# A GRU and an oscillator in one loop on one Trainium2 core: the first base's linear part by itself, pairs and gate work in another order

## What is computed

```python
x = x + GRU(cond_2048, x)                 # h_t from h_{t-1}: gates r, z, candidate n
x = x + Oscillator(cond_2048, cond_2048, x)
x = x + BlockAttention(x)                 # mean over blocks, one attention, layer norm
x = x + Resample(x, cond_2048)

# Oscillator, one time step (Runge-Kutta 4), DT = 0.01:
def derivative(q, p, drive):
    dq = q - q**3 / 3 - p + drive + tanh(q) @ coupling.T + bias
    dp = 0.08 * (q + 0.7 - 0.8 * p)
# dq1..dq4 at q, q + DT/2 dq1, q + DT/2 dq2, q + DT dq3
# q_next = clip(q + DT/6 (dq1 + 2 dq2 + 2 dq3 + dq4), -20, 20); p_next likewise
```

## Time and profile before

| | us |
|---|---|
| median of 3 runs (lowest, highest) | 3536.72 (3535.81, 3536.73) |
| the profiled execution, its own time | 3533.15 |
| its span | 3531.3 |
| busy PE, PEld | 3432.0, 3162.2 |
| busy DVE, ACT, POOL | 2842.0, 2612.1, 1536.1 |
| stage products L1193, first and last start | 210.5, 3390.1 |

### The profile page before, as it was taken

One profiled execution on the slowest core, in us unless ns is written; L12 is line 12 of the kernel. 1 busy time (PEld: TensorE's weight loads), 2 busy tenths in 40 slices (PEclk: granted clock), 3 DMA queues, 4 the chain that ended last, 5 costly groups with the idle time before them and its releaser, 6 DMA issues.

```text
span 3531.3 us, 297078 instructions
## 1 busy us (share of the span) xinstructions
PE 3432.0 (97%) x115469; PEld 3162.2 (90%) x115469; DVE 2842.0 (80%) x20699; ACT 2612.1 (74%) x23713; POOL 1536.1 (43%) x6169
## 2 busy tenths in 40 slices
PE   8989999999999999999999999999999999999978
PEld 4479999999999999999999999999999999999954
DVE  2068888888888888888888888888888888888876
ACT  3257777777777777777777777777777777777752
POOL 0034444444444444444444444444444444444421
PEclk9999999999999999999999999999999999999978
DMA  3000000000000000000000000000000000000001
GB/s 131 24 26 1 1 1 1 1 1 1 1 1 1 1 1 1 1 1 1 1 1 1 1 1 1 1 1 1 1 1 1 1 1 1 1 1 1 1 2 48
DMA packets 9441, 24.35 MB, mean 7 GB/s; under 512 B 556, under 2 KB 600, under 8 KB 8792
## 3 DMA queue, kind: packets, MB, share of 16 engines
q1 hardware_dynamic: 8832, 19.92, 1.5%
q10 hardware_dynamic: 88, 0.02, 0.0%
HBM read 15.75 MB, written 4.19 MB: 6 GB/s over the span
## 4 chain that ended last, share of the span: by engine, by line
PE 68%; DVE 20%; ACT 7%; issue 5%; DVEq 0%; DMA 0%; ACTq 0%; POOL 0%; POOLq 0%
PE psum L1193 38%; PE psum L1150 23%; PE psum L1120 5%; DVE tpart L857 4%; ACT tpart L582 4%; DVE psum L902 2%; ACT tfull L584 2%; DVE qnext L902 2%; DVE psum L888 2%; DVE psum L874 2%; PE psum L1296 1%; DVE q L909 1%; DVE psum L867 1%; DVE gates L791 1%; DVE psum L892 1%
## 5 line engine op out<-in xcount | busy, mean ns | idle before, releaser
L1193 PE MATMUL psum<-tpart,cpl 128*128 128x32 f16 (+1 forms) x65536 | 1965.9, 175 | 30.7 <-DVE tpart L857 11.1
L1193 PEld LDWEIGHTS psum<-tpart,cpl 128*128 128x128 f16 x65536 | 1781.3, 96 | 144.5 <-DVE tpart L857 54.9
L1150 PE MATMUL psum<-hpart,whh 128*128 128x32 f16 x49152 | 1554.1, 176 | 17.8 <-DVE hpart L833 11.4
L1150 PEld LDWEIGHTS psum<-hpart,whh 128*128 128x128 f16 x49152 | 1375.0, 96 | 26.9 <-DVE hpart L833 18.8
L857 DVE TENSOR_TENSOR tpart<-tfull,tpart 128x8 f16<-128x8 f32 x4096 | 675.1, 165 | 226.6 <-ACT tfull L584 94.5
L582 ACT ACTIVATE tpart<-psum 128x8 f16<-128x8 f32 x3072 | 518.4, 175 | 157.7 <-DVE psum L902 91.5
L902 DVE TENSOR_REDUCE psum<-psum 128x8 f32<-128x24 f32 x3072 | 548.7, 190 | 73.2 <-issue 4.0
L584 ACT ACTIVATE tfull<-psum 128x8 f32<-128x8 f32 x3072 | 520.2, 176 | 0.0
L582 ACT ACTIVATE tpart<-qnext 128x8 f16<-128x8 f32 x1024 | 213.3, 208 | 319.5 <-DVE qnext L902 319.5
L546 ACT ACTIVATE qterm<-psum 128x16 f32<-128x16 f32 x3072 | 390.2, 179 | 78.7 <-DVE psum L880 5.4
L392 POOL TENSOR_TENSOR pterm<-pterm,uhat 128x48 f32<-128x48 f32 x512 | 146.3, 286 | 527.3 <-ACT pterm L553 527.3
(11 more groups left out here) (153 smaller groups left out, 4324.5 us busy)
## 6 DMA issues: line engine op xcount, KB each, us to landing
xrow<-in_x_dram SPq DMA_DIRECT2D x4, 1024.0 KB, 12.0
out_dram<-space SPq DMA_DIRECT2D x16, 256.0 KB, 2.0
wih<-in_L_cond_W_ih_dram SPq DMA_DIRECT2D x3, 1024.0 KB, 10.8
space<-in_L_cond_W_hh_dram SPq DMA_DIRECT2D x1, 3072.0 KB, 20.0
space<-in_L_cond_coupling_dram SPq DMA_DIRECT2D x1, 1024.0 KB, 19.2
xrow<-in_cond_dram SPq DMA_DIRECT2D x1, 1024.0 KB, 4.4
wih<-in_L_cond_Wk_dram SPq DMA_DIRECT2D x1, 1024.0 KB, 5.2
wih<-in_L_cond_Wo_dram SPq DMA_DIRECT2D x1, 1024.0 KB, 8.3
```

The lines of the kernel that those rows point to most:

```text
L1150: mm = pe.matmul(gate_out[x][:, :, :, c * B:(c + 1) * B], whh[:, w, k, n * P:(n + 1) * P], copies_in(hpart[:, k, :, :]), start=(c == 0 and ...
L1193: mm = pe.matmul(stage_out[a][:, 0:reps, :, col:col + B], cpl[:, w, k, n * P:(n + 1) * P], copies_in(tpart[:, s % 2, k, :, :])[:, 0:reps, ...
```

## The change

- Stage 0 of a step: `shift_square` goes. A new instruction `linear` forms `linear0 = drive0 - STEP[3]/3 * LINEAR[0] * q1` in SBUF; the cubic is min(q squared, 400) times q1 in one instruction, and the base adds `linear0` in place of `drive0`.
- ACT: `stage_terms(s)` stands directly behind the tanh of half b and ahead of the square in stages 0 and 1 as well (before, behind the square, the sigmoids and a wait for the cubic).
- DVE: `argument(0)` moves from before to behind the row sum of half a in stage 1; `cubic(2)` moves from before `new_high(0)` and `new_h_full(0)` to behind them.
- Waits go: `omzs_ready` in `weigh`, `ka_read` for v > 2 in `new_high`, `qterm_ready` in `sum_stage` and `cubic`.
- PE: ten pairs instead of twelve stand ahead of the wait for the split of half b, and twenty-two behind it.

```diff
@@ ACT, step
-                    if s == 2:
-                        stage_terms(2)
+                    if s < 3:
+                        stage_terms(s)
                     arg, s_next = (in_halves(qnext[:, :]), 0) if s == 3 else (qt, s + 1)
                     if s < 3 or tail <= T:
                         act.activation(in_halves(sq[:, s_next, :]), arg, ACT.Square,
...
                         if gru <= T:
                             sigmoids(0, gru)
-                        act.wait_ge(cub_ready, stage_count(1, now))
-                        stage_terms(0)
-                        if gru <= T:
                             scaled_omz(0, gru)
...
                     if s == 1:
                         if tail <= T:
                             scaled_drive(tail)
-                        act.wait_ge(cub_ready, stage_count(2, now))
-                        stage_terms(1)
@@ DVE
             def weigh(x, v):
 
                 dve.wait_ge(cand_ready[x], v)
-                dve.wait_ge(omzs_ready[x], v)
...
-                    if x == 0:
+                    if x == 0 and v <= 2:
                         dve.wait_ge(ka_read, v)
...
-            def shift_square(v):
-
-                dve.wait_ge(sq_ready[0], v - 1)
-                dve.tensor_scalar(square0, sq[:, 0, :], CLAMP * CLAMP, LINEAR[0], ALU.min, ALU.add).then_inc(shift_ready, 1)
+            def linear(v):
+
+                dve.wait_ge(q1_ready, v)
+                dve.wait_ge(drive0_ready, v)
+                dve.scalar_tensor_tensor(linear0[:, :], q1[:, :], -STEP[3] / 3 * LINEAR[0], drive0[:, :],
+                                         ALU.mult, ALU.add).then_inc(linear_ready, 1)
 
             def cubic(s, v):
 
                 if s == 0:
-                    dve.wait_ge(shift_ready, v)
+                    dve.wait_ge(sq_ready[0], v - 1)
                     dve.wait_ge(q1_ready, v)
-                    dve.tensor_tensor(cub, square0, q1[:, :], ALU.mult).then_inc(cub_ready, 1)
+                    dve.scalar_tensor_tensor(cub, sq[:, 0, :], CLAMP * CLAMP, q1[:, :], ALU.min, ALU.mult).then_inc(cub_ready, 1)
                 else:
 
                     dve.wait_ge(sq_ready[s], v)
-                    if s == 3:
-                        dve.wait_ge(qterm_ready[s], v)
...
                 if s == 0:
-                    dve.wait_ge(drive0_ready, v)
-                    dve.scalar_tensor_tensor(stage_base, in_halves(cub), -STEP[3] / 3, in_halves(drive0[:, :]),
+                    dve.wait_ge(linear_ready, v)
+                    dve.scalar_tensor_tensor(stage_base, in_halves(cub), -STEP[3] / 3, in_halves(linear0[:, :]),
...
                     dve.wait_ge(base_ready, stage_count(s, v))
-                    if s in (1, 2):
-                        dve.wait_ge(qterm_ready[s], v)
@@ DVE, step
                 base(1, now)
                 if gated_step:
                     reset(0, gru)
+
+                sum_stage(1, 0, now)
+                if gated_step:
                     argument(0, gru)
-
-                sum_stage(1, 0, now)
                 sum_stage(1, 1, now)
...
                 split_tanh(2, 1, now, tanh_ready[1][1], now)
-                cubic(2, now)
                 if gated_step:
                     new_high(0, gru)
                     new_h_full(0, gru)
+                cubic(2, now)
                 base(2, now)
...
                     split_tanh(0, 1, tail, tanh_ready[3][1], now)
-                    shift_square(tail)
+                    linear(tail)
                     cubic(0, tail)
                     base(0, tail)
@@ PE, step
                     pe.wait_ge(t_parts[s][0], now)
-                    stage_products(s, k_first, range(HK + 1))
+                    stage_products(s, k_first, range(HK))
+                    stage_products(s, k_first[:1], [HK])
                     pe.wait_ge(t_parts[s][1], now)
                     stage_products(s, k_second, range(HK)).then_inc(stage_mm[s][0], 1)
+                    stage_products(s, k_first[1:], [HK])
                     stage_products(s, k_first, range(HK + 1, K))
                     stage_products(s, k_second, range(HK, K)).then_inc(stage_mm[s][1], 1)
```

More of the change, by code:

```diff
@@ L126, in build @@
         qnext = sb("qnext", [P, KB])
+        linear0 = sb("linear0", [P, KB])
         q1 = sb("q1", [P, KB])
@@ L169, in build @@
         scratch_at = bank + 2 * HC
-        cub, square0, lowest = [psum[:, scratch_at + i * KB:scratch_at + (i + 1) * KB] for i in range(3)]
+        cub, lowest = [psum[:, scratch_at + i * KB:scratch_at + (i + 1) * KB] for i in range(2)]
         stage3 = [triple(0, half), triple(bank + half, half)]
@@ L268, in build @@
         qterm_ready = [sem(f"qterm_ready{s}") for s in range(4)]
-        pterm_ready, shift_ready = sem("pterm_ready"), sem("shift_ready")
+        pterm_ready, linear_ready = sem("pterm_ready"), sem("linear_ready")
         cub_ready = sem("cub_ready")
@@ L915, in _ @@
                                    condT[:, :, :].rearrange("p k b -> p (k b)"), ALU.mult))
-            dve.tensor_scalar(square0, sq[:, 0, :], LINEAR[0], None, ALU.add).then_inc(shift_ready, 1)
-            cubic(0, 1)
+            linear(1)
+            dve.tensor_tensor(cub, sq[:, 0, :], q1[:, :], ALU.mult).then_inc(cub_ready, 1)
             base(0, 1)
```

## The result

| | before | after |
|---|---|---|
| median (lowest to highest) of 20 runs each, us | 3535.04 (3530.74 to 3536.73) | 3540.9 (3537.43 to 3542.89) |
| profiled execution, its span, us | 3533.15, 3531.3 | 3542.03, 3540.2 |
| stage products, first and last start, us | 210.5, 3390.1 | 209.4, 3399.9 |
| mean step, us | 6.210 | 6.232 |
| step without a late instruction, us | 6.144 | 6.1705 |

The ratio is 1.0016 [1.0009, 1.0022]: the changed kernel is slower by 5.9 us, which is under the 0.2% that the prediction had set as its bound. The direction was right, the case was not: it falls under "same", and the forecast of 3557 us was 16 us too high. The nearest of the prediction's cases is rival 2, no change at 3537.

The account below looks back on a forecast made before the run. PE's waits for splits in the half loops were taken as the bound. Gains and losses around the loop summed to +0.04 us a step (6.14 to 6.18), x 512 = +20 us, so median 3557 us, own range 3542 to 3575.

Parts of the forecast that it names:

- same: Whole kernel: outcome within 0.2% (7 us) of the kernel before, given 0.20, beside slower 0.61 and faster 0.19.
- rival 2: Whole kernel: gains in the first base and from the argument's place given back exactly, no change, 3537 us; chance 0.17.
- What bounds the kernel: Products on PE: despite 97% busy, PE stands still 0.6 us a step, 10% of the loop, in waits.
- Stage 0, base: First base of a step: at 0.40 instead of 0.54, sum a 0.68 instead of 0.82, gain 0.14 us.
- Stage 0, b half: Ten pairs make PE wait for the b split: sum b 0.97 instead of 0.92, split b 1.48 instead of 1.55.
- Stage 1, square: Square behind three copies: cubic 1.75 instead of 1.63, sum a 2.23 instead of 2.33, sum b 2.49 instead of 2.54.
- Rival 3: Stage 1: sum b starts 0.21 behind the argument, not 0.14; +0.11 us a step, 3593 us; chance 0.13.
- Stage 2: DVE's row: gates' sum 0.56 behind split b instead of 0.47, so stage 3 starts at 4.63 instead of 4.59.
- Waits that go ... Nothing: DVE's dropped waits for omzs, ka_read and q terms: 0.02 to 0.05 of queue each, counted as no gain.
- What the reordering costs: Stage 2: both additions ahead of the cubic cost 0.10 us, more than the 0.05 gained so far.
- rival 1: Stage 2: the additions don't cost, the 0.05 of split b stays as gain; step 6.09, 3511 us; chance 0.20.
- Rival 4: Stage 0: the new pair order doesn't bring sum a forward at all; already in the sum, without its own price.

Follow-up runs that it names:

- e10: e9 with the gates' sum of half b directly behind the cubic of stage 2, ahead of additions and base; 3431.1 us, ratio 0.973 to the kernel before.
- e3: Kernel before with only the linear part of the first base added; 3478.21 us, ratio 0.983.
- e1: Changed kernel with twelve pairs again, instead of ten, ahead of the wait for the split of half b; 3526.62 us, ratio 0.9963 to the kernel before.
- e6: Kernel before with the linear part and the argument behind the row sum in stage 1; 3474.57 us, ratio 0.9834.
- e8: e6 with the cubic of stage 2 behind the two additions; 3529.09 us, ratio 0.9984 to the kernel before.
- e2: Changed kernel with the square ahead of the copies again, and the copies' and row sums' waits back; 3522.04 us, ratio 0.9953 to the kernel before.
- e9: e6 with the waits for omzs, ka_read (v > 2) and the copies ahead of stage 3's cubic dropped; 3442.67 us, ratio 0.9762 to the kernel before.
- e11: e9 with the copies of q ahead of the square and the row sums' waits for them gone; 3561.17 us, ratio 1.0095 to the kernel before.
- e5: Changed kernel with the cubic of stage 2 in front of the two additions again; 3558.66 us, clean step 6.22 us.
- e12: e6 with only the wait for ka_read in front of new_high of half a dropped; 3453.86 us, ratio 0.9778 to the kernel before.

## Why the prediction was right or wrong

**What bounds the kernel.** Right. PE's idle tenth is made of waits for splits, and e10 took 0.19 us a step out of it without touching a product.

**Stage 0, base.** Right: base 0.40, sum a 0.69 (0.68), stage 1's loads 1.41. e3 gave -0.108 where the walk of the whole had 0.14 at this point; the b half was the next to bind, as said.

**Stage 0, b half.** Right: sum b 0.97, split b 1.47 (1.48), the loads of stage 0 with the gap at the 11th pair. e1: 0.037.

**Stage 1, square.** Right within 0.05: cubic 1.78 (1.75), base 1.99 (1.95), sum a 2.28 (2.23), argument 2.38 (2.35), sum b 2.51 (2.49), split b 3.01 (3.01). Rival 3 wanted sum b 0.21 behind the argument; it is 0.13 (941.74, 941.87). Its other point, the products done at 2.46, was passed by 0.05. One reading of the kernel before was wrong: the argument did not hold sum a there. The third copy ended at 2.20 and sum a came the usual 0.13 behind it, at 2.33, so that moving the argument frees nothing as long as the copies are late (e6, 0.011). The time of sum a came out all the same, because the change moves the copies too.

**Stage 2.** The sum was nearly right, and its account was wrong. The gates' sum stands 0.54 behind the split, not 0.56: the three steps split to addition to addition to cubic take 0.083, 0.082 and 0.076, not 0.09 to 0.10. e8 measured 0.57 in a kernel with the wait for `ka_read` in place, so the row I used was right for a kernel that the change does not make. "Waits that go ... Nothing" is the step that failed. In the order of the changed kernel this one wait is 0.03 in that row (e8 against e2), 15 us over 512 steps. In the terms of my sum the row came out at 0.54 instead of 0.56, which is 10 of the 20 us forecast. In the order of the kernel before, the three waits were worth 0.061 a step (e9). I had counted a wait as the 0.02 to 0.05 of queue time in front of its instruction and set it to zero since something else would be late. In this row DVE's instructions follow one another 0.08 to 0.10 apart, and nothing else was. The wait on omzs was also set not a microsecond before `weigh` but 0.5 to 0.6, which changes nothing.

**What the reordering costs.** The prediction put the 0.10 lost in stage 2 down to the additions in front, and the late square to stage 1 only. The runs put it the other way round. With an early square the reordering costs 0.108 (e8). With the late square it gains: 0.083 at twelve pairs (e11 to e1), 0.05 at ten (e5). The square of stage 2 is ready some 0.2 behind its split, so DVE would stand idle in front of the cubic; the additions fill that gap, which makes the two orders nearly equal (0.55 against 0.54 from split to gates' sum, the first kind of step in e5). The rest of the gain is that the second addition then runs well ahead of GpSimd's `uhat` (0.62 against 0.54, the other kind and e11). The walk used the square "ready at 3.20, before DVE gets there at 3.28" only to show that the cubic would not wait, and never asked what undoing the reordering would give: it would have shown that copies and cubic cost their 0.10 once, not each. I did weigh "the cubic would be waiting for its square anyway" in rival 1, where it stood for a gain of the additions; as a reason why both orders cost about the same it was right.

**The size.** From 0.04 a step to what was measured: the link of stage 2 came out 0.02 shorter (0.54 instead of 0.56). The remaining links miss by up to 0.05 and cancel, so that stage 3 starts at 4.61 (4.63) and the step closes at 6.17 (6.18). Clean it is +0.0265 x 512 = 13.6 us instead of 20. The late instructions cost 0.061 a step instead of 0.066 (mean less clean step), -2.5 us; I had left them as they are. With both, the stage products span 3190.5 instead of 3179.6 us, +10.9. Outside them it is 2.0 us less, which gives the +8.9 of the two spans; the start of the stage products lies anywhere from 207.6 to 210.5 in the fourteen kernels, so I count that as scatter. The last 3 us are no change of the kernel: the profiled execution before lay 1.9 us under the median of its 20 runs, that of after 1.1 over. A sum read to hundredths is good to some 0.02 a step, times 512 some 10 us. That the links cancel is luck. The uncertainty is as much as the effect, and the prediction gave rival 2 too little for it (0.17, "each of its links is read to 0.01 or 0.02").

**Rival 4** (the order of the pairs doesn't bring sum a forward) holds: sum a of stage 0 is at 0.69 with ten pairs and with twelve (e3), held by the base.

**The rule on the drain** (the Trainium skill, "VectorE: DVE Perf Modes", "The DRAIN you can't avoid"). By it, as the prediction gave it, the linear part would have gained nothing. It gained 0.108 a step (e3). The prediction left out what this section of the Trainium skill adds: "A next op that is not held starts earlier". The rows agree with this: linear part and cubic start 0.10 apart, while the base, which reads the cubic's result, starts 0.21 behind it (939.55, 939.76).

## What to carry to other kernels

Ask of each edit not only what it costs, but what it costs with and without the others: here the argument's place is worth 0.22 or 0.01 and the cubic's +0.11 or -0.08, each depending on whether the square stands behind three copies. A change of six parts that comes out at zero may hold a gain of 2.4% (e9) and a loss of about the same size; runs with one part each find it, the whole never shows it. Drop waits that the program's order already covers, above all in front of a row of short dependent instructions, and put what is needed later (the copies) behind what the chain needs first (the square). Where an instruction lasts longer in one kernel than in another, look at what the other engines start within 0.05 us of it, and take the steps of a loop apart before averaging them.

## What the runs showed of the hardware that was not expected

- A wait that was satisfied long ago is not free. One extra semaphore in front of an instruction takes 0.02 us in DVE's queue, two take 0.05. In a row of short instructions the difference arrives in full: 0.03 from the split to the gates' sum (e8 against e2).
- Where an addition on DVE starts 0.02 to 0.05 us behind an instruction of GpSimd, one of the two is longer: DVE's lasts 0.19 to 0.22 us instead of 0.16, or GpSimd's 0.27 instead of 0.22. Where DVE's starts 0.03 or more ahead, both have their usual length. A shift of a few ns decides which of the two it is (0.021 and 0.019 in e12 and e9), and the 0.065 us that DVE loses reaches the step (e12, e5, e11).
- Every four to five steps one DVE instruction starts some 0.2 to 0.35 us late with no releaser. In the changed kernel the cubic of the next stage 0 is one:

```profile
946.08 0.18 DVE L871 SCALAR_TENSOR_TENSOR psum<-sq,q 128x16 f32<-128x16 f32 x1 [0.30 <-issue]
```

Such rows stand in all kernels run; mean and clean step differ by 0.04 to 0.08 us. Counted in DVE's own instructions, waits included (57 a step in the kernel before, 55 in the changed one), the distance from one late instruction to the next is a multiple of 128, to within one or two, in all fourteen traces (128, 256, 384 and so on; 90 to 118 late ones each in 470 steps). So it follows the instruction stream and not the data. What causes it was not tested.
